# Layer norm of the gated-delta output: eight fused VectorE instructions become one subtraction and one multiplication

## What is computed

```python
def _gated_delta(q, k, v, alpha, beta, scale):      # one step for each of 256 tokens, 16 heads
    ...
    err = jnp.einsum('bhvk,bhk->bhv', S, kt) - vt
    S = at[..., None, None] * S - bt[..., None, None] * err[..., None] * kt[:, :, None, :]
    o = jnp.einsum('bhvk,bhk->bhv', S, qt)
...
o = _gated_delta(q, k, v, alpha, beta, scale)
mu = o.mean(-1, keepdims=True)
var = ((o - mu) ** 2).mean(-1, keepdims=True)
o = (o - mu) * jax.lax.rsqrt(var + 1e-05) * ln_w + ln_b
g = jax.nn.sigmoid(x @ Wg).reshape(B, T, H, DV)
o = (o * g).reshape(B, T, H * DV)
return o @ Wo
```

## Time and profile before

| | |
|---|---|
| time, median of three executions | 3970.87 us (3970.86 to 3979.07) |
| profiled execution: device time | 3974.22 us |
| profiled execution: span of its instructions | 3972.4 us |
| TensorE busy, matmul / weight load | 3292.4 us (83%) / 2821.3 us (71%) |
| VectorE busy | 2717.9 us (68%) |
| ScalarE busy | 1866.1 us (47%) |
| GpSimd busy | 1481.3 us (37%) |
| mean DMA rate | 107 GB/s |

### The profile page before, as it was taken

The page is one execution under the profiler, slowest core; times in us unless marked ns, Lnnn a source line. Parts: engine busy times, 40 slices in busy tenths (PEclk is TensorE's granted clock), DMA queues, the critical chain, the costliest instruction groups (busy, mean ns, idle before and its releaser), DMA issues.

```text
span 3972.4 us, 70012 instructions
## 1 busy us (share of the span) xinstructions
PE 3292.4 (83%) x19840; PEld 2821.3 (71%) x19888; DVE 2717.9 (68%) x7066; ACT 1866.1 (47%) x3531; POOL 1481.3 (37%) x1849
## 2 busy tenths in 40 slices
PE   5999999745468999999999899999999999866763
PEld 3777777634357888888888788878888888755652
DVE  4777667674457777777677776777767777666556
ACT  2444444323345555555555555555555555422321
POOL 1101001131444545445454454544545445443222
PEclk9999999877789999999999999999999999888885
DMA  2000000012355454555545555455454555422211
GB/s 78 0 0 0 0 0 0 2 46 98 109 170 157 143 170 143 152 161 145 169 138 162 156 141 172 140 154 161 140 174 124 169 162 145 122 59 74 60 28 42
DMA packets 400206, 423.78 MB, mean 107 GB/s; under 512 B 228692, under 2 KB 278612, under 8 KB 399703
## 3 DMA queue, kind: packets, MB, share of 16 engines
q1 hardware_dynamic: 399830, 419.51, 34.9%
HBM read 276.39 MB, written 143.01 MB: 106 GB/s over the span
## 4 chain that ended last, share of the span: by engine, by line
issue 35%; POOL 21%; PE 19%; DVE 17%; ACT 4%; DMA 2%; POOLq 1%; DVEq 0%; SPq 0%; ACTq 0%
POOL acc L653 7%; POOL inv L670 4%; POOL outer L667 4%; PE bank L1731 3%; POOL oT L709 3%; PE bank L1473 3%; PE bank L1522 2%; DVE acc L1284 2%; DVE row_max L1103 2%; POOL ors L693 2%; DMA k_scratch<-knw 2%; PE bank L1811 2%; PE bank L1681 2%; PE bank L1712 2%; DVE xf L1033 1%
## 5 line engine op out<-in xcount | busy, mean ns | idle before, releaser
L653 POOL TENSOR_TENSOR acc<-acc,shifted 128x510 f32<-128x510 f32 x384 | 504.2, 1314 | 1204.3 <-DVE acc L1284 1204.2
L854 ACT ACTIVATE shifted<-bank,conv_w 128x255 f32<-128x255 f32 x768 | 362.8, 472 | 988.2 <-PE bank L1681 743.1
L1284 DVE SCALAR_TENSOR_TENSOR acc<-bank,conv_w,acc 128x254 f32<-128x254 f32 (+1 forms) x1536 | 629.6, 471 | 128.4 <-ACT acc L856 128.4
L1681 PE MATMUL bank<-x_k,w_kq 128*128 128x256 f32 x2048 | 495.8, 388 | 36.7 <-DVE acc L1284 31.7
L1681 PEld LDWEIGHTS bank<-x_k,w_kq 128*128 128x128 f32 x2048 | 380.4, 195 | 83.9 <-DVE acc L1284 34.9
L856 ACT ACTIVATE acc<-bank,conv_b,conv_w 128x256 f32<-128x256 f32 x768 | 433.9, 565 | 0.0
L1731 PE MATMUL bank<-y,GT 128*128 128x128 f32 x2048 | 285.7, 283 | 97.9 <-DVE y L1329 84.6
L1712 PE MATMUL bank<-kq 128*128 128x256 f32 x1024 | 266.0, 408 | 103.1 <-ACT kq L866 67.4
L1731 PEld LDWEIGHTS bank<-y,GT 128*128 128x128 f32 x2048 | 261.5, 194 | 118.1 <-DVE y L1329 97.5
L1712 PEld LDWEIGHTS bank<-kq 128*128 128x128 f32 x1024 | 198.6, 203 | 155.5 <-ACT kq L866 77.2
L1811 PE MATMUL bank<-w_o,oT 128*128 128x256 f32 x1024 | 258.4, 410 | 39.5 <-POOL oT L709 39.5
(11 more groups left out here) (235 smaller groups left out, 6998.5 us busy)
## 6 DMA issues: line engine op xcount, KB each, us to landing
abc<-decay_scratch SPq DMA_DIRECT2D x64, 512.0 KB, 4.4
q_scratch<-kq SPq DMA_DIRECT2D x64, 512.0 KB, 4.7
L_scratch<-LT SPq DMA_DIRECT2D x64, 512.0 KB, 2.7
M_scratch<-MT SPq DMA_DIRECT2D x64, 512.0 KB, 3.9
LTm<-L_scratch SPq DMA_DIRECT2D x64, 512.0 KB, 4.5
kqm<-q_scratch SPq DMA_DIRECT2D x64, 512.0 KB, 3.6
MTm<-M_scratch SPq DMA_DIRECT2D x128, 256.0 KB, 3.5
k_scratch<-knw SPq DMA_DIRECT2D x64, 258.0 KB, 4.8
```

The lines of the kernel that those rows point to most:

```text
L653: pool.tensor_tensor(dst, dst, shifted[:, u % 2, :, 1:], ALU.add).then_inc(Z["sumk" if u < 4 else "sumv"], 1)
L854: act.activation(shifted[:, u % 2, i % 2, 1:], pj[:, 0:SEQ - 1], ACT.Copy, scale=conv_w[:, kind, bass.ds(head, 1), TAPS - 2:TAPS - 1].rear ...
L1284: dve.scalar_tensor_tensor(out=acc[:, kind, i, t:], in0=pj[:, 0:SEQ - t], scalar=wcol, in1=acc[:, kind, i, t:], op0=ALU.mult, op1=ALU.add) ...
L1681: mm = pe.matmul(dst[:, i * SEQ:(i + 1) * SEQ], w[:, k, head * DK:(head + 1) * DK], x[:, k, :], start=(k == 0), stop=(k == CT - 1))
```

## The change

VectorE's instruction list changes and nothing else. The eight `tensor_scalar` of `normalise` go. In their place, `moments_of_out` now ends with one `tensor_tensor` that subtracts the means, read with a stride of zero along each tile, from all eight tiles (128 x 1024 elements), in place; `normalise` waits for `ors` and for that subtraction's own semaphore `ocen`, and multiplies all eight tiles by `ors` with one more `tensor_tensor`, in place.

```diff
-            "r1", "oi", "op0", "oev", "op1", "oadd", "ostat", "omom", "ovar", "ors", "on",
+            "r1", "oi", "op0", "oev", "op1", "oadd", "ostat", "omom", "ocen", "ovar", "ors", "on",
...
                     ins.then_inc(Z["omom"], 1)
                     dve.wait_ge(Z["omom"], past(n + 1))
                     dve.tensor_scalar(ovar[:], omom[:, :, 1], EPS, None, ALU.add).then_inc(Z["ovar"], 1)
+                    dve.tensor_tensor(of, of, omom[:, :, 0:1].broadcast_to([P, PROBS, DK]), ALU.subtract).then_inc(Z["ocen"], 1)
 
                 def normalise():
                     dve.wait_ge(Z["ors"], past(n + 1))
-                    for m in range(PROBS):
-                        ins = dve.tensor_scalar(of[:, m], of[:, m], omom[:, m, 0:1], ors[:, m:m + 1], ALU.subtract, ALU.mult)
-                    ins.then_inc(Z["on"], 1)
+                    dve.wait_ge(Z["ocen"], past(n + 1))
+                    dve.tensor_tensor(of, of, ors[:].unsqueeze(2).broadcast_to([P, PROBS, DK]), ALU.mult).then_inc(Z["on"], 1)
```

## The result

The changed kernel takes 4039.41 us (median of four, 4034.79 to 4047.51) against 3970.86 for the kernel before: 1.0173 times as long, 95% interval 1.0149 to 1.0196. Slower was forecast, but by 19 us, and it is 68.5; the time lies outside the forecast range of 3968 to 4010.

The account below looks back on a forecast made before the run. TensorE's first products were taken to bound each slot, reached through VectorE's own path or through L653, ScalarE and TensorE. +27.2 us over 54 slots less 8 in the last ten gave +19: 3990 us, range 3968 to 4010.

Parts of the forecast that it names:

- the one on the multiplication: VectorE behind Uw: issued at 3.44, held by L653 till 4.65, giving VectorE back at 5.8 instead of 7.1.
- the term on L653: GpSimd's L653, behind conv(3) and beside Uw, ends at 4.65 us after ovar instead of 3.60.
- the detour: Path from conv(3) through L653, ScalarE's tap(5) and copy of S, TensorE's from_state to r1; starts 1.05 later, decides every slot.
- Products decide: TensorE's first products (L1712) set the next slot's start; a microsecond lost before them is lost for good.
- it doesn't reach the next slot: Rival: delay in slots 4k+2 doesn't set the next slot's start, so their 13.8 drop out; 3976 us, chance 0.16 including mixtures.
- The subtraction holds VectorE 1.14: Right behind ovar there is no idle time to hide it, so conv(3) starts at 1.26 instead of 0.12.
- The price of the subtraction alone: Later products over the 54 slots that have them, with the start of L653's path delayed: +27.2 us together.
- By kinds: Slots by n modulo four, products later by 0.20 (4k), 0.73 (4k+1), 1.06 (4k+2), 0.03 us (4k+3) each.
- The power: GpSimd's instruction ahead of L653: ends between 1.90 undisturbed and 2.99 if held by the subtraction; no effect on the sum.
- The last ten slots: Subtraction covered by VectorE's wait for ScalarE, multiplication shorter than the eight instructions: 0.91 in nine slots, -8 us.
- L653 ahead of `Uw`: Rival: GpSimd's L653 overtakes Uw, whose margin is 0.16 us, so products come later; 4009 us, chance 0.10.
- Faster: Rival: the subtraction doesn't hold back conv(3), and VectorE-bound slots shorten; -33 us, 3938 us, chance 0.10.

Follow-up runs that it names:

- mul_late: The changed kernel with the multiplication moved behind conv(4); 1.0010 times the kernel before.
- no_sub: The changed kernel without the subtraction and its semaphore, so not computing the whole layer norm; 0.9967 times the kernel before.
- sub_then_eight: The changed kernel with its early subtraction, but the multiplication again as eight tensor_scalar of 128 x 128; 1.0075 times the kernel before.
- no_mul: The changed kernel with a one-element memset in place of the multiplication, early subtraction kept; 1.0004 times the kernel before.
- both_late: The changed kernel with subtraction and multiplication both moved behind conv(4); 3947.6 us, 0.9916 times the kernel before.
- gap_before_uw: The changed kernel with a one-element memset ahead of Uw, so Uw and the multiplication still follow each other; 1.0041 times the kernel before.
- gap_memset: The changed kernel with a one-element memset between Uw and the multiplication; 3990.8 us, 1.0024 times the kernel before.

## Why the prediction was wrong

**The step that failed** is the one on the multiplication: "It is issued at 3.44, is held by L653 till 4.65". In 43 of the 54 slots it was not held; it held L653. With it fell the term on L653, "ends at 3.52 + 1.13 = 4.65": it ended at 5.72, so the detour was 2.12 late and not 1.05. This is shown by the changed trace, by mul_late and by the two memset kernels, in which L653 ends at 4.57 to 4.59 and the 54 slots lengthen by 13.5 to 21.8 (21.8 to 27.6 up to the products, where 27.2 was forecast). In the eleven slots in which L653 did go first, it ended at 5.39 to 5.41 in nine and at 5.29 and 5.31 in the other two, against 5.41 forecast.

**Why I missed it.** I asked for the race between L653 and `Uw`, and took the one between L653 and what follows `Uw` as settled, since L653 had won it in each slot. I read "L653 has started" as "L653 has the port", and the prediction gives no other reason. In the rows of before the margin stood to be read: L653 starts at 2002.48, the first `tensor_scalar` at 2003.00, 0.52 later. In the change `Uw` no longer follows its own input but `conv(3)`, and L653 follows `conv(3)` too, by 0.08 to 0.09; my own numbers, 2.99 and 3.44, gave 0.45 for the new margin. I had nothing that says who goes first at a margin of 0.45, and should have put "the multiplication goes first" among the rivals: 4.59 + 1.13 + 6.76 = 12.48, which is 1.07 later in each of the 43 slots where the multiplication went first, 46 us more. The margin alone would not have told: at 0.52 the multiplication loses (no_sub), at 0.44 a `tensor_scalar` loses too (sub_then_eight); it took the smaller margin and the two-input instruction together. Why the order turns there is open.

**Right, point by point.** Products decide and their delay carries over: from `ovar` to products the 54 slots lost 70.5 us in all, from products to the next `ovar` they won 5.8, within the scatter of this part between kernels (from -11.8 to +5.3). The rival that it doesn't reach the next slot is out. The subtraction holds VectorE 1.14, `conv(3)` starts 1.22 after `ovar` (forecast 1.26), it is not covered. The price of the subtraction alone, forecast at +27.2, is +24.5 up to the products in no_mul; over the whole of the 54 slots it is +13.5, because the other part came out 11.0 shorter, which I can't attribute. L653 to products stayed 6.76 where this path decides: 6.76 or 6.77 in 44 of the 54 slots of the change (6.42 in six of the first and last slots, 7.5 in four of the kind 4k+1). By kinds, the forecast of +2.8 (4k), +10.2 (4k+1), +13.8 (4k+2) and +0.4 (4k+3) is near what mul_late has up to the products, +1.2, +9.6, +11.9 and -0.8; the change has +17.0, +13.0, +26.5 and +13.9. The power ended at 2.81, within its bounds, and `conv(3)` at 2.86, so L653 waited for `conv(3)`, not for the power.

**The last ten slots**: forecast -8, measured -6.3, in one trace each. By the price from the Trainium skill, "VectorE: DVE Perf Modes", section on the TRN2 errata, it would have been +1; the row of before decided rightly. The prediction didn't take in what the Trainium skill says there, below the table: the 58 cycles are too few, and the fixed term measured is about 150. With 150, at the 0.96 GHz of the same section, as an estimate, eight instructions of 214 cycles against one of 1174 make 1.78 us against 1.22, and the nine slots win 5.

**The rivals.** L653 ahead of `Uw` didn't happen; `Uw` won with 0.16. The page that I set beside it, the Trainium skill, "SBUF — State Buffer" (who interferes with whom), says that whoever issues first gets the shared port pair for the whole instruction; the prediction put "starts" for it. By starts in the trace it is not so here: L653 starts 0.43 to 0.44 us before the multiplication and loses. If the rule holds for requests at the port, the recorded starts are some 0.44 us off against each other: GpSimd's request comes later than its recorded start, VectorE's earlier than its own, or both. The Trainium skill, "Perfetto Trace Analysis" (summary of the profiler window per engine type), says that a VectorE instruction's recorded window leaves out the start of its prefetch; no run here shows whether that is the reason, or how much of the 0.44 us it is. "Faster" had the right idea in the wrong place: moved out of the way of `conv(3)` and L653, the same two instructions win 0.8%.

## What to carry to other kernels

- Where two engines share a port, price both outcomes of every meeting, and read the margin of each race in the trace before the change. An order that holds in all slots may hold by some 80 ns (0.52 against 0.44 here), and an edit elsewhere that ties both to the same event uses it up.
- Work that is not urgent, but long and with two SBUF inputs, belongs where its engine waits for something, not where a short instruction of the neighbour carries the chain. The place was worth more here than the number of instructions.
- Halves of a change need not add up: -13.3 and +13.5 made +64.7.
- Compare an expectation with the part of the slot that it speaks of: both_late met what was expected of the 54 slots while one kind of slot got 14.8 us worse.

## What the runs showed of the hardware

- A VectorE `tensor_tensor` with both inputs in SBUF holds even GpSimd's power over eight elements: 2.55 us in place of 1.65, each of the 64 times (2541 to 2559 ns).
- The order of L653 and a `tensor_tensor` behind it on VectorE turns at about 0.44 us of recorded head start. In the changed kernel VectorE is first 42 times at 434 to 440 ns and once at 443, GpSimd 11 times at 442 to 444; with a memset ahead of `Uw` (gap_before_uw), at 447 to 458, GpSimd 54 times; with a memset between (gap_memset) GpSimd 54 times at 440 to 455. That the head start decides, and not the kind of slot or the memset, is not shown.
- The loser waits for all of the winner. L653 (1.26 us undisturbed) ends 1.12 to 1.14 after a multiplication that went first, the multiplication (1.22) 1.08 after an L653 that did.
- A `tensor_scalar` lost at 436 to 440 ns, where a `tensor_tensor` won. Why was not found.
- Records of VectorE need not keep the order of its list: a memset of one element is recorded 0.01 to 0.03 us behind the start of the instruction that follows it (both memset kernels).
